# Attention loop: the stage lists of the five engines laid out in another order

## The chip, the cores and the metric

The kernel runs on one core of a Trainium2 chip. The metric is the time of one execution on the device in microseconds, the median of several runs. Each engine (TensorE or PE, VectorE or DVE, ScalarE or ACT, GpSimd or POOL, SyncE or SP, which here only issues DMAs) works through its own instructions in order; they meet only through semaphores.

## What is computed

32 sequences of 512 tokens go through one transformer layer with 256 channels. Cut to what matters:

```python
h = take(emb, x) + (take(lora_A, x) @ lora_B.T) * 2              # embedding with LoRA
n = layernorm(h)
q, k, v = split(n @ Wqkv + bqkv)                                 # 16 heads of 16 channels
local  = softmax(q @ k.T / 4, masked to |i - j| <= 64) @ v
glob   = softmax(q @ k[:64].T / 4) @ v[:64]
gate   = sigmoid(n @ Wg + bg)
h = h + ((1 - gate) * local + gate * glob) @ Wout + bout
f = layernorm(h)
probs, idx = top_2(softmax(f @ router_w.T))                      # 8 experts, weights normalised
# rank of each (token, choice) within its expert, in order over all tokens; a capacity per expert
out = h + sum_k probs_k * expert[idx_k](f)                       # silu(f @ w1) @ w2, kept ranks only
```

## The kernel before

A setup block (to about 50 us) brings weights and tables into place. Then one block runs the attention loop for all 32 sequences, and a last block runs the experts over the slots of a table that the loop has filled. The change lies in the loop alone.

The loop is written as *stages*. ORDER has one list for each engine; an entry is (flag, stage, argument). The function order walks over i from -3 to 34 and yields each entry for sequence i + REL[flag], where that is one of the 32; REL gives old -3, past -2, prev -1, cur 0, nxt 1, far 2, next 3. So an engine works on up to seven sequences at once, and its list is the one thing that sets the order of its work. All waits are on counts that follow from stage and sequence, wherever the stage stands.

The stages, as the text names them (the numbers are the arguments; g is one of four groups of heads):

- *embed, lora 0-1* (PE; ACT and DVE behind them): tokens' LoRA rows are transposed (L824), multiplied (L830) and added to the gathered rows into h (DVE L1138). embed waits for all 8 *gathers* of its sequence (POOL L570, L573). *hold 0-3* (POOL L602) and *hold*, *hb* (SP) keep h for later. *stats1, std1* (ACT square root, L946), *rstd1, scale1* are the first layernorm; *zgate 0-1* (DVE L1175, L1180), *gate*, *gate1*, *gate2*, *gates* the gate.
- *xn_t 0-1, qk 0-3, values 0-2* (PE L837, L843, L781): projections. q and k are split into three bf16 terms: ACT qk (L933), DVE qk (L1099, frees the PSUM bank), ACT qk2 (L940), POOL qk3 (L596), and written out and loaded again by SP (*qk_write*, *load*).
- *max 0-19* (PE scores L685, L701, L707; DVE row maxima L966, L970), five for each g; *cut (g, 0-3)* (DVE) splits the maxima, *m_rows g* (PE L793, ACT L907) turns them, *m_out, m_in* (SP) bring them behind Q. Each max on PE waits for the DVE part of the max before it.
- *exp 0-19* (PE scores L727, L734; ACT exponentials L879, L883): each exp on PE waits for the ACT part of the exp before it. *sel* (POOL L556 and L558, two instructions each) cuts the local ones to the band. *out 0-11* (PE L755, L760) multiplies by the values; *evac* (ACT L889) empties the result.
- *mix 0-3*: PE transposes (L803, both PSUM banks of psX), DVE takes reciprocal, coefficient and product (L1065, L1070, L1075), POOL adds (L589). *attn_t 0-1* (PE L810) waits for all four. *project 0-1* (PE L817, DVE L1120) gives h1; *stats2, std2* (ACT square root, L943), *rstd2, scale2 0-3* (DVE L1161) the second layernorm; *x2_t, router* (PE L850, L857) the router; *residual* (POOL L606), *y*, *x2* (SP) the results.
- *top 0-8, rank 0-5* (DVE): the two best experts and the ranks. top 3 is L1009; top 5 to 8 add up bf16 counts (L1020); *ahead* (PE L864, L865) sums over partitions. rank 4 (L1050 to L1052) writes slot_i and entry and first waits until all *scatters* (POOL L580) of the sequence before have landed; rank 5 is L1055. scatter 0-7 write the slot table and wait for rank 4 of their own sequence.

The PSUM banks of psX (two) go in turn to the PE stages other than exp, max and out, so a stage waits for whoever emptied the bank two stages earlier: embed waits for DVE's project 0.

Of the kernel before, what the change touches and what calls it, by code (L numbers as in the profile page):

```python
# [90 lines left out]
def build(nc, x, emb, lora_a, lora_b, wqkv, bqkv, wout, bout, wg, bg, rw, w1, w2, y):  # L91
# [20 lines left out]
    with outer:  # L112
# [241 lines left out]
        with ExitStack() as mem:  # L354
# [34 lines left out]
            mix = tmp("mix", [P, 2, 2, H, HD])  # L389
# [71 lines left out]
                ("prev", "out", 11), ("cur", "m_rows", 1), ("cur", "values", 2), ("cur", "max", 11), ("nxt", "xn_t", 0),  # L461
                ("nxt", "xn_t", 1), ("cur", "exp", 0), ("cur", "max", 12), ("nxt", "qk", 0), ("nxt", "qk", 1), ("cur", "max", 13),
                ("nxt", "qk", 2), ("nxt", "qk", 3), ("cur", "exp", 1), ("cur", "max", 14), ("prev", "mix", 0), ("cur", "exp", 2),
                ("cur", "max", 15), ("cur", "exp", 3), ("prev", "mix", 1), ("cur", "max", 16), ("cur", "exp", 4), ("cur", "out", 0),
                ("cur", "max", 17), ("prev", "mix", 2), ("cur", "exp", 5), ("cur", "out", 1), ("cur", "exp", 6), ("cur", "max", 18),
# [6 lines left out]
                ("prev", "x2_t", 0), ("nxt", "max", 6), ("cur", "exp", 16), ("cur", "out", 8), ("nxt", "max", 7), ("prev", "x2_t", 1),  # L472
                ("cur", "exp", 17), ("nxt", "max", 8), ("prev", "router", None), ("cur", "exp", 18), ("nxt", "values", 0),
                ("nxt", "max", 9), ("cur", "exp", 19), ("nxt", "values", 1), ("cur", "out", 9), ("nxt", "max", 10), ("cur", "out", 10),
            )
            ORDER["act"] = (
                ("nxt", "qk2", 1), ("prev", "evac", (3, 0)), ("prev", "evac", (3, 1)), ("nxt", "qk", 2), ("nxt", "qk", 3),
                ("nxt", "qk2", 2), ("cur", "exp", 1), ("nxt", "qk2", 3), ("cur", "exp", 2), ("cur", "exp", 3), ("cur", "exp", 4),
                ("cur", "exp", 5), ("cur", "exp", 6), ("cur", "m_rows", 2), ("cur", "exp", 7), ("cur", "evac", (0, 0)),
                ("cur", "evac", (0, 1)), ("cur", "exp", 8), ("cur", "m_rows", 3), ("prev", "attn_t", 0), ("prev", "attn_t", 1),  # L480
                ("cur", "exp", 9), ("far", "embed", None), ("cur", "exp", 10), ("cur", "evac", (1, 0)), ("nxt", "gate", None),
                ("cur", "exp", 11), ("cur", "exp", 12), ("prev", "std2", None), ("cur", "exp", 13), ("cur", "evac", (1, 1)),
                ("cur", "exp", 14), ("cur", "exp", 15), ("nxt", "m_rows", 0), ("cur", "exp", 16), ("prev", "x2_t", 0),
                ("prev", "x2_t", 1), ("cur", "exp", 17), ("cur", "exp", 18), ("cur", "evac", (2, 0)), ("cur", "evac", (2, 1)),
                ("far", "std1", None), ("cur", "exp", 19), ("nxt", "values", 0), ("nxt", "values", 1), ("nxt", "m_rows", 1),
                ("nxt", "values", 2), ("far", "xn_t", 0), ("far", "xn_t", 1), ("far", "qk", 0), ("nxt", "exp", 0),
                ("prev", "weights", None), ("far", "qk", 1), ("far", "qk2", 0),
            )
            ORDER["dve"] = (
                ("nxt", "rstd1", None), ("cur", "cut", (1, 0)), ("cur", "kg", 1), ("cur", "cut", (1, 1)), ("old", "rank", 3),  # L490
                ("nxt", "scale1", 0), ("cur", "cut", (1, 2)), ("cur", "gate1", None), ("cur", "kg", 2), ("cur", "cut", (1, 3)),
                ("old", "rank", 4), ("cur", "max", 10), ("nxt", "scale1", 1), ("nxt", "scale1", 2), ("nxt", "scale1", 3),
# [1146 lines left out]
```

## Time and profile before

| | us |
|---|---|
| median of 3 runs (3838.16 to 3849.77) | 3839.25 |
| the profiled execution | 3837.03 |
| its span | 3834.7 |
| PE busy | 3447.8 (90%) |
| DVE busy | 2241.1 (58%) |
| ACT busy | 1988.1 (52%) |
| POOL busy | 2337.5 (61%) |
| attention loop, about | 50 to 2249 |
| one sequence in the middle | 65.9 |

The busy shares are means over two unlike parts: in the loop (up to about 2250 us) all engines are between 60 and 90% busy, behind it TensorE alone is nearly full. Windows of the loop show more than the page's shares. In a timeline row the bracket tells how long the engine stood idle before it and what released it.

### The profile page before, as it was taken

How to read it: one execution, taken by the hardware profiler on the slowest of the kernel's cores; microseconds unless marked ns; L12 is line 12 of the kernel's file. 1: busy time of each engine (PE TensorE's matmuls, PEld its weight loads, DVE VectorE, ACT ScalarE, POOL GpSimd, SP SyncE). 2: the span in 40 equal slices, each digit the busy share in tenths (PEclk: the TensorE clock that was granted, in tenths of full speed). 3: DMA queues.
4: the chain of work that ended last, by engine and by line, in shares of the span. 5: the costliest groups of instructions: out<-in, count | busy, mean ns of one | idle time of the engine just before them, and what ended most of it. 6: DMA issues, size and time to landing. Idle time of an engine off the chain costs nothing. (4 is left out here: it accounts for less than half of the span.)

```text
span 3834.7 us, 117863 instructions
## 1 busy us (share of the span) xinstructions
PE 3447.8 (90%) x47729; PEld 2806.7 (73%) x47729; DVE 2241.1 (58%) x5390; ACT 1988.1 (52%) x3118; POOL 2337.5 (61%) x2663
## 2 busy tenths in 40 slices
PE   2889898889899898888889739999999999999998
PEld 1565565656565555566565539999999999999998
DVE  3577777777867777777777534443444444343343
ACT  0566665666666666656666524444444444444443
POOL 5467777777777777777776644444444455444443
PEclk7899999999999999999999869999999999999999
DMA  4444444444444544444544223232323333222222
GB/s 138 146 143 154 129 146 144 131 148 137 148 134 146 139 147 134 145 146 130 152 135 148 66 86 59 52 66 49 72 48 70 58 60 74 45 51 45 46 45 41
DMA packets 242539, 398.30 MB, mean 104 GB/s; under 512 B 34572, under 2 KB 150748, under 8 KB 242044
## 3 DMA queue, kind: packets, MB, share of 16 engines
q1 hardware_dynamic: 168540, 297.43, 24.9%
q0 software_dynamic: 70512, 91.16, 13.5%
q8 instruction: 345, 5.65, 0.7%
q10 hardware_dynamic: 3008, 2.95, 0.2%
q14 instruction: 134, 1.10, 0.1%
HBM read 198.55 MB, written 192.88 MB: 102 GB/s over the span
## 5 line engine op out<-in xcount | busy, mean ns | idle before, releaser
L1351 POOL DMA_INDIRECT out_y<-out_t,tok_out x264 | 424.9, 1609 | 732.6 <-DMA out_y<-out_t,tok_out 397.9
L1497 ACT ACTIVATE act<-psS 128x512 f32<-128x512 f32 x528 | 316.0, 599 | 870.7 <-PE psS L1425 870.7
L1559 DVE TENSOR_TENSOR h_lo<-act,h_hi 128x512 fp32r<-128x512 f32 x528 | 367.4, 696 | 553.0 <-ACT h_hi L1498 553.0
L879 ACT ACTIVATE pl<-psS 128x896 f32<-128x896 f32 x512 | 468.4, 915 | 281.2 <-PE psS L727 275.5
L1460 PE MATMUL psO<-w_hi,h_hi 128*128 128x256 f32 x2112 | 598.5, 283 | 0.0
L1460 PE MATMUL psO<-w_lo,h_hi 128*128 128x256 f32 x2112 | 588.7, 279 | 0.0
L1460 PE MATMUL psO<-w_hi,h_lo 128*128 128x256 f32 x2112 | 587.6, 278 | 0.0
L556 POOL TENSOR_SCALAR_AFFINE_SELECT pl<-pl 128x512 f32<-128x512 f32 x512 | 354.8, 693 | 361.8 <-ACT pl L879 360.8
L1425 PE MATMUL psS<-xg_hi,w_hi 128*128 128x256 f32 x1984 | 551.6, 278 | 0.0
L1425 PE MATMUL psS<-xg_hi,w_lo 128*128 128x256 f32 x1984 | 551.3, 278 | 0.0
L1425 PE MATMUL psS<-xg_lo,w_hi 128*128 128x256 f32 x1984 | 551.2, 278 | 0.0
L966 DVE TENSOR_REDUCE negm<-psS 128x4 f32<-128x640 f32 x512 | 416.8, 814 | 196.1 <-PE psS L701 190.8
L1460 PEld LDWEIGHTS psO<-w_hi,h_hi 128*128 128x128 f32 x2112 | 397.1, 188 | 0.0
L1460 PEld LDWEIGHTS psO<-w_lo,h_hi 128*128 128x128 f32 x2112 | 397.0, 188 | 0.0
L1460 PEld LDWEIGHTS psO<-w_hi,h_lo 128*128 128x128 f32 x2112 | 395.5, 187 | 0.0
L1425 PEld LDWEIGHTS psS<-xg_hi,w_hi 128*128 128x128 f32 x1984 | 375.0, 189 | 0.0
L1425 PEld LDWEIGHTS psS<-xg_lo,w_hi 128*128 128x128 f32 x1984 | 372.5, 188 | 0.0
L1425 PEld LDWEIGHTS psS<-xg_hi,w_lo 128*128 128x128 f32 x1984 | 372.4, 188 | 0.0
L1591 DVE TENSOR_SCALAR out_t<-psO,wt_all 128x256 f32<-128x256 f32 x264 | 127.7, 484 | 356.5 <-PE psO L1460 355.5
L558 POOL TENSOR_SCALAR_AFFINE_SELECT pl<-pl 128x512 f32<-128x512 f32 x512 | 328.1, 641 | 0.0
L1498 ACT ACTIVATE h_hi<-psS 128x512 fp32r<-128x512 f32 x528 | 313.1, 593 | 0.0
L1316 POOL DMA_INDIRECT xg<-x_rows,tok_in x245 | 258.5, 1055 | 74.9 <-issue 73.7
(229 smaller groups left out, 7741.8 us busy)
## 6 DMA issues: line engine op xcount, KB each, us to landing
qk_scr<-qk SPq DMA_DIRECT2D x64, 768.0 KB, 4.0
Q<-qk_scr SPq DMA_DIRECT2D x128, 384.0 KB, 4.7
K<-qk_scr SPq DMA_DIRECT2D x128, 384.0 KB, 5.5
qk_scr<-qk SPq DMA_DIRECT2D x64, 512.0 KB, 3.4
qk_scr<-qk SPq DMA_DIRECT2D x64, 256.0 KB, 3.5
h_rows<-held SPq DMA_DIRECT2D x32, 512.0 KB
hb<-h_rows SPq DMA_DIRECT2D x32, 512.0 KB
out_y<-h SPq DMA_DIRECT2D x32, 512.0 KB
```

Of the source, the lines that this page charges most:

```text
L556: pool.affine_select(out=cols[:, :, 0:P], in_=cols[:, :, 0:P], compare_op=ALU.is_ge, fill=0.0, base=0, pattern=[[0, 4], [1, P]], channel_m ...
L558: pool.affine_select(out=cols[:, :, P:WIN], in_=cols[:, :, P:WIN], compare_op=ALU.is_ge, fill=0.0, base=0, pattern=[[0, 4], [-1, P]], chan ...
L879: act.activation(pl[:, v, half, :, lo:hi], psS[:, 0:2, lo:hi], ACT.Exp, scale=SCALE).then_inc(exp_done, 1)
L966: dve.tensor_reduce(negm[:, g, 0, v, :, 2 * half:2 * half + 2], psS[:, 2:4, 0:2 * BAND].rearrange("p a (q u) -> p a q u", u=BAND), AX.X, A ...
L1316: pool.indirect_dma_start(out=rows[:, s, :], out_offset=None, in_=x2_rows[:, :], in_offset=bass.IndirectOffsetOnAxis(ap=tokens[:, s:s + 1] ...
L1351: pool.indirect_dma_start(out=y[:, :], in_=out_t[:, tile.out, s, :], in_offset=None, out_offset=bass.IndirectOffsetOnAxis(ap=tok_out[:, ti ...
L1425: last = pe.matmul(psS[:, f // 2, (f % 2) * 256:(f % 2) * 256 + cols], w[:, tile.par, k, fs], x[:, k, 0:cols], start=(k == 0 and n == 0), ...
L1460: last = pe.matmul(psO[:, s, 0:D], h_[:, f, ts], w[:, tile.par, f, :], start=(f == 0 and n == 0), stop=(f == FT - 1 and n == 2))
L1497: act.activation(act32[:, b, :, 0:cols], src, ACT.Silu)
L1498: act.activation(h_hi[:, 2 * b:2 * b + 2, 0:cols], src, ACT.Silu).then_inc(silu_done, 1)
L1559: dve.tensor_tensor(h_lo[:, 2 * b:2 * b + 2, 0:cols], act32[:, b, :, 0:cols], h_hi[:, 2 * b:2 * b + 2, 0:cols].bitcast(F32), ALU.subtract) ...
L1591: dve.tensor_scalar(out_t[:, tile.out, s, :], psO[:, s, 0:D], wt_all[:, bass.ds(tile.h0 + s, 1)], None, ALU.mult).then_inc(out_done, 1)
```

## The change

All five lists of ORDER are replaced by lists with the same stages in another order. The periods are also cut at other places, which changes only the flags. Nothing else in the kernel changes. The parts that the text below speaks of (whole new list of DVE but for its middle, the first half of PE's and POOL's, the region of std2 in ACT's):

```diff
             ORDER["pe"] = (
...
-                ("nxt", "xn_t", 1), ("cur", "exp", 0), ("cur", "max", 12), ("nxt", "qk", 0), ("nxt", "qk", 1), ("cur", "max", 13),
-                ("nxt", "qk", 2), ("nxt", "qk", 3), ("cur", "exp", 1), ("cur", "max", 14), ("prev", "mix", 0), ("cur", "exp", 2),
...
-                ("cur", "m_rows", 2), ("cur", "exp", 7), ("cur", "max", 19), ("prev", "mix", 3), ("cur", "out", 2), ("cur", "exp", 8),
-                ("cur", "out", 3), ("cur", "m_rows", 3), ("prev", "attn_t", 0), ("prev", "attn_t", 1), ("cur", "exp", 9),
-                ("past", "ahead", None), ("prev", "project", 0), ("prev", "project", 1), ("far", "embed", None), ("nxt", "max", 0),
-                ("cur", "exp", 10), ("cur", "out", 4), ("nxt", "max", 1), ("cur", "exp", 11), ("far", "lora", 0), ("nxt", "max", 2),
-                ("cur", "exp", 12), ("cur", "out", 5), ("nxt", "max", 3), ("cur", "exp", 13), ("far", "lora", 1), ("nxt", "max", 4),
-                ("cur", "exp", 14), ("cur", "out", 6), ("cur", "out", 7), ("nxt", "max", 5), ("cur", "exp", 15), ("nxt", "m_rows", 0),
...
+                ("nxt", "xn_t", 1), ("cur", "exp", 0), ("cur", "max", 12), ("nxt", "qk", 0), ("cur", "exp", 1), ("nxt", "qk", 1),
+                ("cur", "exp", 2), ("nxt", "qk", 2), ("cur", "max", 13), ("nxt", "qk", 3), ("cur", "exp", 3), ("cur", "max", 14),
+                ("prev", "mix", 0), ("cur", "exp", 4), ("cur", "max", 15), ("cur", "out", 0), ("prev", "mix", 1), ("cur", "exp", 5),
+                ("cur", "max", 16), ("cur", "exp", 6), ("cur", "m_rows", 2), ("cur", "max", 17), ("prev", "mix", 2),
+                ("cur", "max", 18), ("cur", "exp", 7), ("cur", "out", 1), ("prev", "mix", 3), ("cur", "max", 19), ("cur", "exp", 8),
+                ("cur", "out", 2), ("cur", "exp", 9), ("cur", "out", 3), ("past", "ahead", None), ("cur", "m_rows", 3),
+                ("nxt", "max", 0), ("prev", "attn_t", 0), ("prev", "attn_t", 1), ("nxt", "max", 1), ("cur", "exp", 10),
+                ("prev", "project", 0), ("nxt", "max", 2), ("cur", "exp", 11), ("prev", "project", 1), ("far", "embed", None),
+                ("cur", "out", 4), ("cur", "exp", 12), ("nxt", "max", 3), ("far", "lora", 0), ("cur", "exp", 13), ("nxt", "max", 4),
+                ("cur", "out", 5), ("far", "lora", 1), ("nxt", "max", 5), ("cur", "exp", 14), ("cur", "out", 6), ("cur", "out", 7),
...
             ORDER["act"] = (
...
+                ("prev", "exp", 11), ("nxt", "embed", None), ("prev", "exp", 12), ("past", "std2", None), ("prev", "exp", 13),
...
             ORDER["dve"] = (
...
+                ("old", "rank", 1), ("cur", "max", 0), ("old", "rank", 2), ("cur", "max", 1), ("old", "rank", 3), ("prev", "kg", 3),
+                ("cur", "kg", 0), ("old", "rank", 4), ("cur", "max", 2), ("past", "project", 0), ("past", "project", 1),
+                ("past", "stats2", 0), ("past", "stats2", 1), ("cur", "max", 3), ("old", "rank", 5), ("nxt", "lora", 0),
+                ("past", "rstd2", None), ("cur", "max", 4), ("past", "scale2", 0), ("cur", "cut", (0, 0)), ("past", "scale2", 1),
+                ("cur", "cut", (0, 1)), ("cur", "max", 5), ("past", "scale2", 2), ("nxt", "lora", 1), ("past", "scale2", 3),
+                ("cur", "max", 6), ("cur", "cut", (0, 2)), ("cur", "cut", (0, 3)), ("cur", "max", 7), ("nxt", "stats1", 0),
...
+                ("nxt", "scale1", 2), ("past", "top", 3), ("cur", "max", 10), ("past", "top", 4), ("nxt", "scale1", 3),
+                ("cur", "gate1", None), ("cur", "max", 11), ("cur", "kg", 1), ("nxt", "zgate", 0), ("cur", "kg", 2),
+                ("cur", "max", 12), ("past", "top", 5), ("past", "top", 6), ("nxt", "qk", 0), ("nxt", "qk", 1), ("cur", "max", 13),
+                ("nxt", "qk", 2), ("past", "top", 7), ("nxt", "qk", 3), ("cur", "max", 14), ("prev", "mix", (0, 0)),
...
             ORDER["pool"] = (
...
+                ("old", "scatter", 6), ("prev", "mix", 3), ("cur", "sel", 7), ("old", "scatter", 7), ("far", "gather", 7),
+                ("nxt", "hold", 2), ("cur", "sel", 8), ("past", "scatter", 0), ("nxt", "hold", 3), ("cur", "sel", 10),
...
+                ("prev", "residual", 3), ("nxt", "sel", 0), ("far", "qk3", 0), ("nxt", "sel", 1), ("far", "qk3", 1),
+                ("nxt", "sel", 2), ("far", "qk3", 2), ("far", "qk3", 3), ("next", "gather", 4), ("next", "gather", 5),
+                ("nxt", "sel", 3), ("past", "scatter", 5), ("nxt", "sel", 5), ("cur", "mix", 0), ("cur", "mix", 1),
+                ("nxt", "sel", 6), ("far", "hold", 1), ("next", "gather", 6), ("cur", "mix", 2),
             )
             ORDER["sp"] = (
...
+                ("cur", "y", None), ("cur", "x2", None), ("next", "qk_write", (0, 0)), ("far", "m_in", 1),
```

## Rows read from the trace of the kernel before

**Rows 1.** Windows: busy us of PE, PEld, DVE, ACT, POOL; granted clock; DMA.

```profile
1226.59:1292.50 65.91, 59.79 (x1077) 39.39 (x1076) 49.63 (x127) 40.82 (x60) 49.01 (x65) 0.95 0.50 140
2200.00:3834.00 1634.00, 1551.18 (x13309) 1546.26 (x13308) 655.41 (x1326) 679.78 (x1237) 763.49 (x586) 0.97 0.30 57
```

**Rows 2.** Timeline of PE (start, length, what): exp 0 and embed.

```profile
1226.59 0.46 PE L727 MATMUL psS<-Q,K 102*32 102x96 bf16 x16
...
1261.32 0.60 PE L824 MATMUL psX<-ident,la 128*16 128x128 f32 x4
```

**Rows 3.** Window from qk to the last mix; DVE and POOL in it.

```profile
1230.10:1254.60 24.50, 20.44 (x373) 12.50 (x375) 22.90 (x47) 13.82 (x22) 19.61 (x24) 0.93 0.52 175
...
1230.80 1.21 DVE L1175 TENSOR_TENSOR xn_wg<-xn,wg_b 128x1024 f32<-128x1024 f32 x1
...
1234.45 0.97 DVE L1009 TENSOR_TENSOR onehot<-iota,top_f 128x64 f32<-128x64 f32 x1
...
1246.96 2.40 DVE L1020 TENSOR_TENSOR before<-before,chosen 128x8 bf16<-128x8 bf16 x1
...
1248.71 0.62 POOL L558 TENSOR_SCALAR_AFFINE_SELECT pl<-pl 128x512 f32<-128x512 f32 x1
```

**Rows 4.** PE at max 19; window behind it, columns as in the first group.

```profile
1250.15 0.79 PE L707 MATMUL psS<-K,Q 96*128 96x64 bf16 x16 [1.69 <-DVE negm L966]
1250.75 1.95 PE L803 MATMUL psX<-ident,o_t 128*128 128x128 f32 x8
...
1250.60:1254.10 3.50, 3.50 (x23) 2.07 (x24) 2.55 (x11) 0.60 (x1) 1.50 (x2) 0.53 0.79 228
```

**Rows 5.** Timeline: ACT from exp 12 to exp 13, PE at exp 14.

```profile
1266.09 0.92 ACT L879 ACTIVATE pl<-psS 128x896 f32<-128x896 f32 x1 [0.94 <-PE psS L727]
1267.03 1.28 ACT L943 ACT_TABLE_LOAD   x1
...
1269.93 0.92 ACT L879 ACTIVATE pl<-psS 128x896 f32<-128x896 f32 x1
...
1270.99 1.06 PE L734 MATMUL psS<-Q,KG 102*64 102x512 bf16 x4 [1.73 <-ACT pl L879]
```

**Rows 6.** Timeline of POOL: qk3, two selects; grouped: mix (mean ns of one).

```profile
1233.07 2.27 POOL L596 TENSOR_TENSOR qk<-qk_rest,qk 128x512 bf16<-128x512 f32 x2
...
1240.80 0.63 POOL L556 TENSOR_SCALAR_AFFINE_SELECT pl<-pl 128x512 f32<-128x512 f32 x1
...
1241.98 0.64 POOL L556 TENSOR_SCALAR_AFFINE_SELECT pl<-pl 128x512 f32<-128x512 f32 x1
...
L589 POOL TENSOR_TENSOR attn<-mix 128x256 f32<-128x256 f32 x28 | 20.1, 731 | 15.0 <-DVE mix L1075 14.8
```

**Rows 7.** Timeline: last scatter and slot_i at the end; last gather and embed at the start.

```profile
2234.06 0.97 POOL L580 DMA_INDIRECT slot_table<-entry,slot_i  x1 [0.30 <-issue]
...
2238.47 0.17 DVE L1050 TENSOR_TENSOR slot_i<-slot,over 128x8 int32<-128x8 f32 x1 [9.46 <-DMA slot_table<-entry,slot_i]
...
60.18 0.95 POOL L573 DMA_INDIRECT emb_t<-in_L_tok_emb_weight,id_cur  x1 [0.30 <-issue]
...
63.01 1.02 PE L824 MATMUL psX<-ident,la 128*16 128x128 f32 x4 [19.10 <-DMA emb_t<-in_L_tok_emb_weight,id_cur]
```

**Rows 8.** DVE and PE behind embed: project, max 0 to out 4, x2_t; window.

```profile
1261.52 0.69 DVE L1120 TENSOR_TENSOR h<-psX,hb 128x512 f32<-128x512 f32 x1 [1.03 <-PE psX L817]
1261.85 0.46 PE L685 MATMUL psS<-K,Q 96*32 96x96 bf16 x16
1262.47 0.99 PE L755 MATMUL psO<-pl,V 128*32 128x256 f32 x16
1263.98 0.82 DVE L966 TENSOR_REDUCE negm<-psS 128x4 f32<-128x640 f32 x1 [0.68 <-PE psS L701]
...
1275.62 0.66 PE L850 MATMUL psX<-ident,x 128*128 128x128 f32 x4
...
1261.50:1272.80 11.30, 9.57 (x236) 6.09 (x238) 10.04 (x24) 8.89 (x12) 8.90 (x16) 0.92 0.29 88
```

More of the change, by code:

```diff
@@ L473, in build @@
-                ("cur", "exp", 17), ("nxt", "max", 8), ("prev", "router", None), ("cur", "exp", 18), ("nxt", "values", 0),
-                ("nxt", "max", 9), ("cur", "exp", 19), ("nxt", "values", 1), ("cur", "out", 9), ("nxt", "max", 10), ("cur", "out", 10),
+                ("prev", "exp", 19), ("prev", "out", 9), ("cur", "values", 1), ("cur", "max", 10), ("prev", "out", 10),
+                ("cur", "m_rows", 1), ("prev", "out", 11), ("cur", "values", 2), ("cur", "max", 11), ("nxt", "xn_t", 0),
@@ new lines, in build @@
+                ("cur", "out", 4), ("cur", "exp", 12), ("nxt", "max", 3), ("far", "lora", 0), ("cur", "exp", 13), ("nxt", "max", 4),
+                ("cur", "out", 5), ("far", "lora", 1), ("nxt", "max", 5), ("cur", "exp", 14), ("cur", "out", 6), ("cur", "out", 7),
+                ("cur", "exp", 15), ("nxt", "max", 6), ("prev", "x2_t", 0), ("prev", "x2_t", 1), ("cur", "exp", 16),
+                ("nxt", "max", 7), ("nxt", "m_rows", 0), ("cur", "out", 8), ("cur", "exp", 17), ("prev", "router", None),
@@ L480, in build @@
[L480 to L487, printed above, removed]
+                ("prev", "m_rows", 3), ("past", "attn_t", 0), ("past", "attn_t", 1), ("prev", "exp", 10), ("prev", "evac", (0, 1)),
@@ L488, in build @@
+                ("cur", "exp", 8), ("cur", "evac", (0, 0)), ("cur", "exp", 9),
             )
             ORDER["dve"] = (
[L490 to L492 removed]
@@ L501, in build @@
-                ("cur", "gates", None), ("prev", "mix", (3, 1)), ("cur", "cut", (3, 2)), ("cur", "kg", 3), ("cur", "cut", (3, 3)),
-                ("prev", "mix", (3, 2)), ("past", "rank", 0), ("past", "rank", 1), ("prev", "project", 0), ("prev", "project", 1),
-                ("nxt", "max", 0), ("nxt", "max", 1), ("prev", "stats2", 0), ("nxt", "max", 2), ("prev", "stats2", 1),
-                ("far", "lora", 0), ("nxt", "max", 3), ("prev", "rstd2", None), ("prev", "scale2", 0), ("nxt", "kg", 0),
@@ L509, in build @@
+                ("cur", "cut", (3, 1)), ("prev", "mix", (3, 2)), ("cur", "cut", (3, 2)), ("cur", "cut", (3, 3)),
+                ("past", "rank", 0),
             )
             ORDER["pool"] = (
-                ("cur", "sel", 8), ("nxt", "hold", 1), ("nxt", "hold", 2), ("nxt", "hold", 3), ("cur", "sel", 10), ("cur", "sel", 11),
-                ("old", "scatter", 4), ("cur", "sel", 12), ("cur", "sel", 13), ("next", "gather", 0), ("next", "gather", 1),
-                ("next", "gather", 2), ("old", "scatter", 5), ("old", "scatter", 6), ("old", "scatter", 7), ("cur", "sel", 15),
@@ L514, in build @@
-                ("prev", "residual", 0), ("cur", "sel", 16), ("cur", "sel", 17), ("next", "gather", 3), ("prev", "residual", 1),
-                ("cur", "sel", 18), ("prev", "residual", 2), ("prev", "residual", 3), ("nxt", "sel", 0), ("far", "qk3", 0),
-                ("far", "qk3", 1), ("past", "scatter", 0), ("far", "qk3", 2), ("far", "qk3", 3), ("nxt", "sel", 1), ("nxt", "sel", 2),
-                ("nxt", "sel", 3), ("next", "gather", 4), ("cur", "mix", 0), ("cur", "mix", 1), ("next", "gather", 5), ("nxt", "sel", 5),
@@ L518, in build @@
-                ("nxt", "sel", 6), ("cur", "mix", 2), ("next", "gather", 6), ("next", "gather", 7), ("cur", "mix", 3), ("nxt", "sel", 7),
-                ("past", "scatter", 1), ("far", "hold", 0), ("past", "scatter", 2), ("past", "scatter", 3),
+                ("old", "scatter", 6), ("prev", "mix", 3), ("cur", "sel", 7), ("old", "scatter", 7), ("far", "gather", 7),
+                ("nxt", "hold", 2), ("cur", "sel", 8), ("past", "scatter", 0), ("nxt", "hold", 3), ("cur", "sel", 10),
+                ("cur", "sel", 11), ("past", "scatter", 1), ("cur", "sel", 12), ("cur", "sel", 13), ("past", "scatter", 2),
```

49 lines of the change are left out of this document (25 added, 24 removed).

## The prediction, made before the changed kernel was seen

> **What bounds the kernel now.** I read the page's first lines, then the stretches, then one sequence of the attention loop as a timeline of each engine. The loop over 32 sequences ends near 2250 us; the expert stage behind it has TensorE busy nearly throughout and is not touched [rows 1]. One sequence in the middle takes 65.9 us from its first scores, exp 0 at 1226.59, to the next sequence's [rows 1, 2]. TensorE is busy 59.8 of them at a mean granted clock of 0.95, so 6.1 us are waits and, at full clock, some 3.3 us more would fall away: 9.4 us a sequence, 290 us in all, is the most that an order can give. No other engine is full: DVE 49.6, POOL 49.0, ACT 40.8 us [rows 1]. What counts is who waits for whom, and where.
>
> Two places carry most of the loss. First, from the q and k projections to the last mix DVE is busy 22.9 of 24.5 us, while TensorE has 20.4 at a clock of 0.93: there DVE sets the pace [rows 3]. It does work there that nothing near waits for: zgate's product (1.21 us), top 3 (0.97), rank 5, and an 8-element addition, top 7, that lasts 2.40 us, from 1246.96 until the fourth of four select instructions on POOL ends (1249.33) [rows 3]. Behind it max 19 starts after 1.69 us of idle TensorE, and the mix after it takes 1.95 us, at the lower of the two clock levels (0.53 of full over 3.5 us, 1.2 GHz nearly throughout) [rows 4]. Second, ACT takes a square root between exp 12 and exp 13: two table loads of 1.28 us, and so exp 14 on TensorE starts after 1.73 us of idle [rows 5].
>
> **The change part by part.** Every stage, wait and buffer stays; no instruction is added. So the sum is one of positions. I count from exp 0 of a sequence.
>
> *First stretch, exp 0 to embed: before 34.7 us* (1226.59 to 1261.32 [rows 2]). The new DVE list takes zgate 0 ahead of it, zgate 1 between max 16 and 17, top 3 and 4 ahead, and rank 5 behind max 3; of the rows named 2.2 us leave the full piece (1.21 + 0.97), and rank 5 and the short parts 1, 2 and 4 of top with them. DVE then is no longer what is late; POOL is. In the new list POOL runs, from its first qk3 (6.5 us after exp 0 [rows 6]) on, without a pause: 4 qk3 of 1.14, the selects 1, 2, 3, 5, 6, 7 at 1.18 from start to start, 4 additions of mix and 1 of hold (of the same size) at 0.73 [rows 6], and 3 gathers and 3 scatters at 0.97 + 0.30 of issue [rows 7]. That is 4.6 + 7.1 + 3.7 + 7.6 = 23.0 us in all, and scatter 7 of the sequence three back is done on POOL at 29.5.
>
> Here the order makes a wait that costs nothing today. rank 4 of the next sequence overwrites the entries, and so waits until all eight scatters have landed. Before, it stands at the end of the period, with POOL four selects, four residuals and a gather beyond scatter 7; now it stands behind max 1, ahead of max 2 and both projects. The landing has a row: the last of eight scatters ends on POOL at 2235.03, and DVE's slot_i starts at 2238.47, 3.4 us later [rows 7]. So rank 4 can start at 32.9, and its three operations (0.17 and two like it, overlapped: some 0.4), max 2 (0.82) and project 0 (0.69 [rows 8]) end at 34.8. Behind DVE in rank 4 stand max 2, for which TensorE waits at max 3, and project 0, which frees embed's bank: embed at 34.8. A second path ends close by: embed also waits for the last gather, now right behind scatter 7, at 29.5 + 1.27 + 1.9 = 32.7 (gather end 61.13 to embed 63.01 [rows 7]). Embed thus comes when it did, 34.8 against 34.7, but max 0, exp 10, max 1, exp 11 and max 2 are now ahead of it. A max with an exp takes 0.62 us there (1261.85 to 1262.47 [rows 8]), so this is 0.62 + 0.62 + 0.4 = 1.6 us of work already done.
>
> *Second stretch, embed to the next exp 0: before 31.2 us.* Off come the 1.6. Off comes the wait at exp 14: between exp 13 and exp 14 TensorE had lora 1 and max 4, and now has max 4, out 5, lora 1 and max 5, about 3 us, while the root waits where it did; what is late next there is nothing, since exp 13 ends on ACT about 3.8 us after exp 12 (1267.01 to 1270.85 [rows 5]) and TensorE gets to exp 14 later than that: -1.7. On comes a wait at x2_t. From project 1 to the fourth scale2 DVE is busy 10.0 us today [rows 8]; the new list has three max (0.82 each) and a copy for KG less there, and rank 5 and one max more: some 8.8 us, which with small waits of its own (0.7, my guess) puts x2 at 44.3. TensorE gets there from embed in 14.3 us today (1261.32 to 1275.62 [rows 8]); less the 1.6, the 1.7 and the 1.6 that the low clock costs (below) that is 9.4, so 44.2, and I take +0.4 for the uncertainty of both. The other moves here (out 11 behind m_rows 1, router behind exp 17, evac (3, 0) ahead of the next sequence) have covers of over a microsecond on both sides and I cost them at nothing; if the covers fail, they are the 0.3 us waits that stand in such places now.
>
> *Clock and stalls.* The clock falls behind the 1.7 us idle of max 19 (0.53 over 3.5 us [rows 4]), and the stretch behind embed has 0.92 on the whole [rows 8]. A stretch like the first costs 3.5 x (1 - 0.53) = 1.6 us. A shorter idle may leave the clock up (-1.6 a sequence), and DVE's short operations will now meet other POOL work: top 7 stands beside qk3 and selects, the first coefficient of mix beside qk3. No row shows the new meetings. They are bounded below by 0 and above by the 2.40 us row once in the piece that carries the path plus 1.14 (a whole qk3) once, so 0 to 3.5; I take 0.8 for both together, since POOL and not DVE is late there by the sum above, and the clock gives part back.
>
> By the Trainium skill (SBUF — State Buffer, section "Who interferes with whom") a DVE instruction with two SBUF inputs and a GpSimd one that reads SBUF exclude each other, and the second to issue waits until the first is done. By that rule top 7 would wait for one select, 0.64 us, or one qk3, 1.14 [rows 6]; the row in [rows 3] shows the exclusion, but a wait through four selects. By the rule alone the upper end of the stalls would be 2.3 and not 3.5 us.
>
> Sum for one sequence: 34.8 + 31.2 - 1.6 - 1.7 + 0.4 + 0.8 = 63.9, against 65.9: -2.0. All lists are full for about 28 of the 32 sequences (the flags span seven, and the first and last have stages missing): -56 us.
>
> *The end of the loop.* Here the same edit gains. Before, rank 4 of the last but one sequence comes behind the last one's router, so the last one's slot_i waits 9.46 us for those scatters [rows 7]. The new list has it ahead of the last one's project; its scatters 0 to 4 go out before and 5 to 7 just behind the last residuals, and the wait shrinks to some 0.5: -9 us. The start shows no such thing: the same gathers and loads bound it, 0 +- 3.
>
> The profiled execution took 3837.0 us, its span 3834.7; the median of the runs is 3839.25, 2.2 more. 3837.0 - 56 - 9 = 3772, as a median 3774.
>
> **The rivals.**
> (a) *More goes than the sum says.* If POOL keeps up with the new queue (today it has pauses in it), the two large waits simply go, with what the low clock costs behind the first: 65.9 - 1.7 - 1.6 - 1.7 and 0.8 of stalls is 61.7. 28 x -4.2 - 9 = -127: 3712. For it: DVE and ACT are both relieved where they were late. Against: rank 4 stands there, and its price has a row.
> (b) *Given back.* The wait of DVE in rank 4, with all that is queued behind it, takes the place of that at max 19 and exp 14: period 65.9, and only the end gains: 3830.
> (c) *Slower.* The same wait is longer than what was won. It works through POOL: each microsecond by which mix 3 is late there (DVE's mix stalled by selects, as top 7 was) moves sel 7, scatter 7, its landing, rank 4, max 2 and embed one for one. It decides from 2.3 us of lateness a sequence beyond my sum (2.0, and 0.3 for the end). With the upper bound of the stalls (3.5 instead of 0.8) and the x2_t wait a little longer (0.2) the period is 66.8: 28 x 0.9 - 9 = +16: 3855. For it: DVE finishes its mixes within a microsecond or two of POOL. Against: DVE sheds 4 us there.
> (d) *It doesn't do what it says.* The lists could be mere rotations. They are not: rank 4 goes some 40 places up on DVE against its neighbours.
>
> **How the numbers follow.** Forecast 0.50, (a) 0.20, (b) 0.13, (c) 0.15, (d) or other 0.02. A measurement of this kernel can tell about 0.3% (12 us) from no change; (b) lies within. Faster 0.72, same 0.13, slower 0.15. The range takes in most of (a) and all of (b), and leaves (c)'s upper part: 3710 to 3855.
>
> **What would show it.** Right: period 63 to 65; no idle of over 1 us at max 19 or exp 14; DVE idle before slot_i in each sequence with the landing of slot_table as its releaser, or POOL without a pause from qk3 to scatter 7; embed about 35 us after exp 0; the 9.46 us wait gone; granted clock in the loop at or over 0.96. Wrong: rank 4 waiting over 3 us (then (c)), or embed well ahead of 34 us (then (a)); or DMA-bound loads of Q and K, which my sum takes as in time because their places on SP move by less than their present slack.

## The result, and the profile after

The changed kernel takes 3718.18 us (median of 4 runs, 3716.92 to 3719.01), the kernel before 3844.51 (4 runs, 3838.16 to 3853.59): ratio 0.967, 95% interval 0.965 to 0.969. I had forecast 3774, so the sign and the range hold. The range was wide, from a clear gain to no gain at all, and the point is 56 us too high: the gain is 126 us and not 65, about that of rival (a), 3712.

The experiments ran elsewhere. The record names chip 13 for the first eight runs (I call it the second chip: the kernel before takes 4042 to 4045 us there and the changed one 3786) and chip 0 for the last four, from the spread run on (the third chip: the kernel before takes 4028, the changed one was not run). For the two kernels above it names no chip; I call theirs the first. The kernels are the same to the letter, so I put the 5% between 3844 and 4042 down to the chips, which is an inference. I keep them apart: the first for what the change did in my prediction's terms, the others for causes.

Where the 118 us between the two profiled executions went (first chip; exp 0 of the first and of the last sequence, then the end):

| | before | after | difference |
|---|---|---|---|
| start to the first exp 0 | 126.5 | 124.3 | -2.2 |
| first exp 0 to the last | 2013.3 | 1912.7 | -100.6 |
| last exp 0 to the end of the span | 1694.9 | 1679.5 | -15.4 |
| one sequence (mean of 22 in the middle) | 66.05 | 62.23 | -3.82 |

The same window of the kernel before, from the first exp 0 to the last (us from and to, length, busy time of PE, PEld, DVE, ACT, POOL, granted clock, DMA share, GB/s):

```profile
126.50:2139.80 2013.30, 1800.78 (x33238) 1197.66 (x33241) 1505.04 (x3828) 1261.41 (x1814) 1483.37 (x1969) 0.97 0.47 142
```

And of the kernel after, with one sequence in the middle, which answers to [rows 1]:

```profile
124.30:2037.00 1912.70, 1775.01 (x33238) 1157.86 (x33241) 1576.79 (x3842) 1239.79 (x1815) 1470.06 (x1973) 0.99 0.53 149
1233.65:1295.73 62.08, 57.48 (x1078) 37.53 (x1077) 52.35 (x128) 40.30 (x60) 48.69 (x65) 1.00 0.53 150
```

DVE is busier by 72 us in a shorter loop, and it costs nothing: its share is not what sets the time. The granted clock went from 0.97 to 0.99. In the clock records of the loop TensorE stood at 1.2 GHz for 133 us before (31 stretches, 30 of them in or right behind the wait at max 19 or at exp 14) and for 34 us after (9 stretches). That is 67 us of full-clock time lost before and 17 after.

The timeline of TensorE in that sequence of the kernel after, for [rows 2, 4, 5, 8]: mix 1, exp 6, mix 3, embed and x2_t (start, length, what, then in brackets the idle time before it and what ended it):

```profile
1248.11 1.09 PE L807 MATMUL psX<-ident,o_t 128*128 128x128 f32 x8 [0.53 <-DVE mix L1079]
...
1250.61 0.46 PE L731 MATMUL psS<-Q,K 102*32 102x96 bf16 x16 [0.62 <-ACT pl L883]
...
1256.68 1.09 PE L807 MATMUL psX<-ident,o_t 128*128 128x128 f32 x8 [1.35 <-DVE mix L1079]
...
1269.77 0.60 PE L828 MATMUL psX<-ident,la 128*16 128x128 f32 x4
...
1279.36 1.09 PE L854 MATMUL psX<-ident,x 128*128 128x128 f32 x8
```

The waits of 1.69 us at max 19 and of 1.73 at exp 14 are gone, embed comes 36.1 us after exp 0, and x2_t starts with no idle. The longest wait left is a new one, 1.35 us at mix 3. DVE and POOL show where it comes from and what became of rank 4:

```profile
1252.65 0.67 POOL L562 TENSOR_SCALAR_AFFINE_SELECT pl<-pl 128x512 f32<-128x512 f32 x1
1253.25 1.44 POOL L593 TENSOR_TENSOR attn<-mix 128x256 f32<-128x256 f32 x2
1253.97 1.93 DVE L1074 TENSOR_TENSOR coef<-rsum,gates 128x32 f32<-128x32 f32 x1
1254.62 0.65 POOL L560 TENSOR_SCALAR_AFFINE_SELECT pl<-pl 128x512 f32<-128x512 f32 x1
1255.21 0.64 POOL L562 TENSOR_SCALAR_AFFINE_SELECT pl<-pl 128x512 f32<-128x512 f32 x1
...
1263.00 1.01 POOL L584 DMA_INDIRECT slot_table<-entry,slot_i  x1 [0.16 <-issue]
...
1267.48 0.17 DVE L1054 TENSOR_TENSOR slot_i<-slot,over 128x8 int32<-128x8 f32 x1
```

The product coef for part 2 (32 elements, mix (2, 1) in the list) took 1.93 us, through POOL's second mix addition and two selects. It stands where top 7 stood before ([rows 3], 2.40 us). Scatter 7 ends at 1264.01 (1263.00 + 1.01), rank 4 runs at 1267.48: 3.5 us later.

At the end of the loop (DVE, the last slot_i; before it waited 9.46 us [rows 7]):

```profile
2126.36 0.17 DVE L1054 TENSOR_TENSOR slot_i<-slot,over 128x8 int32<-128x8 f32 x1 [0.35 <-DMA slot_table<-entry,slot_i]
```

### The profile page after: what moved, and what is told of

Same layout as the page of the kernel before. It is cut to its first block and busy times, and to the rows that moved or that the text cites. A ratio compares the mean times of both kernels' runs of the same rounds, so it can differ in the third digit from the quotient of the medians.

```text
span 3716.5 us, 117861 instructions
## 1 busy us (share of the span) xinstructions
PE 3422.8 (92%) x47729; PEld 2766.8 (74%) x47729; DVE 2313.3 (62%) x5390; ACT 1964.8 (53%) x3116; POOL 2321.8 (62%) x2663
## 5 line engine op out<-in xcount | busy, mean ns | idle before, releaser
L560 POOL TENSOR_SCALAR_AFFINE_SELECT pl<-pl 128x512 f32<-128x512 f32 x512 | 330.0, 644 | 162.6 <-ACT pl L883 157.3
L562 POOL TENSOR_SCALAR_AFFINE_SELECT pl<-pl 128x512 f32<-128x512 f32 x512 | 328.9, 642 | 0.0
L584 POOL DMA_INDIRECT slot_table<-entry,slot_i x256 | 258.2, 1008 | 98.2 <-DVE entry L1056 55.9
```

The source lines that it names most:

```text
L560: pool.affine_select(out=cols[:, :, 0:P], in_=cols[:, :, 0:P], compare_op=ALU.is_ge, fill=0.0, base=0, pattern=[[0, 4], [1, P]], channel_m ...
L562: pool.affine_select(out=cols[:, :, P:WIN], in_=cols[:, :, P:WIN], compare_op=ALU.is_ge, fill=0.0, base=0, pattern=[[0, 4], [-1, P]], chan ...
L584: pool.indirect_dma_start(out=table[:, :], in_=entry[:, q, k, :], in_offset=None, out_offset=bass.IndirectOffsetOnAxis(ap=slot_i[:, q, k:k ...
```

## The experiments

**What had to be told apart.** Theory: the loop gained by the two waits and, as a price of its own, by the clock that no longer falls behind them; the early rank 4 matters at the end only. Rivals: the waits alone; a floor elsewhere. The first group of four runs overturned the plan, because on the second chip other waits dominate.

**The cover of exp 14 alone** (kernel before, TensorE's list):

```diff
-("nxt","max",3), ("cur","exp",13), ("far","lora",1), ("nxt","max",4), ("cur","exp",14), ("cur","out",6), ("cur","out",7), ("nxt","max",5)
+("nxt","max",3), ("cur","exp",13), ("nxt","max",4), ("cur","out",5), ("far","lora",1), ("nxt","max",5), ("cur","exp",14), ("cur","out",6), ("cur","out",7)
```

> The kernel before with one piece of the new TensorE list: max 4, out 5, lora 1 and max 5 stand ahead of exp 14 (before: lora 1 and max 4). Nothing else moves. Theory (waits and the clock behind them are two prices): the 1.7 us wait at exp 14 goes in about 29 sequences, -50 us, and with it the some ten stretches at half clock that follow it, 10 x 1.7 = -17 us: 3839 - 67 = 3772. Rival one (my prediction's own step, the wait only, the clock comes down elsewhere): -1.7 x 28 = -48, 3791. Rival two (given back: with exp 14 on time the next wait, x2_t or exp 15, takes it over): 3825 or more.

Measured: 4063.4 us against 4045.5, ratio 1.005 (1.002 to 1.007). Both theories of a gain miss. Rival two gave the number (nothing gained) but not the mechanism: exp 14 isn't on time, it starts at 46.9 us of the sequence (median) where it was at 43.0. What holds it is the other engine's list, shown with the spread run with both moves below.

**top 7 and 8 behind max 19 alone** (kernel before, DVE's list):

```diff
-("prev","mix",(2,2)), ("past","top",7), ("cur","max",18), ("past","top",8), ("cur","max",19)
+("prev","mix",(2,2)), ("cur","max",18), ("cur","max",19), ("past","top",7), ("past","top",8)
```

> The kernel before with one move on DVE: top 7 and top 8 stand behind max 19 instead of around max 18. Nothing else moves. Theory: the 2.4 us addition no longer holds max 18 and 19, TensorE's 1.7 us wait at max 19 goes (-47 us over 28 sequences) and with it some twenty stretches at half clock, 48 us of TensorE's time in all: 3839 - 95 = 3744. Rival one (the wait only): 3792. Rival two (the locked addition just moves: mix 3 and the transposes behind it wait instead, and the clock falls there): 3825 or more.

Measured: 4035.3, ratio 0.998 (0.996 to 0.999). Nearly nothing, and the trace of the kernel before on this chip (below) says why: there the same top 7 takes 1.24 us and not 2.40, since POOL's selects fall differently, and max 19 waits 0.2 us at most. So rival two's number holds here for want of a wait to take away, not by its mechanism. What the move would give on the first chip isn't shown by it.

**Both** (the two edits above together):

> The kernel before with both moves: exp 14 covered on TensorE, top 7 and 8 behind max 19 on DVE. Four stages of some 190 change places. Theory: the two places are independent and all the loop's gain is in them: 3839 - 67 - 95 = 3677, below the changed kernel's 3718. Rival one (a common floor: DVE from the q and k projections to the last mix holds the period near the 62.2 us of the changed kernel): 31 x -2.7 = 3755. Rival two (clock: half clock comes back behind any of the smaller waits once the large ones are gone): only the two waits, 3839 - 97 = 3742.

Measured: 4057.8, ratio 1.004 (1.002 to 1.005). All three expectations miss, for the reasons of the first two runs.

**The early rank undone** (changed kernel; DVE's rank 4 and 5 behind router, POOL's scatters 0 to 4 later):

```diff
-("cur","kg",0), ("old","rank",4), ("cur","max",2) ... ("cur","max",3), ("old","rank",5) ... ("past","router",None)
+("cur","kg",0), ("cur","max",2) ... ("cur","max",3) ... ("past","router",None), ("old","rank",4), ("old","rank",5)
-("cur","sel",18), ("next","gather",2), ("past","scatter",4), ("next","gather",3)
+("cur","sel",18), ("past","scatter",0), ("next","gather",2), ("past","scatter",1), ("next","gather",3), ("past","scatter",2)
```

> The changed kernel with the early rank undone: rank 4 and 5 stand behind router on DVE, and scatters 0 to 4 move some 20 us later on POOL, as they must. Theory (the early rank matters at the end only): the loop keeps its 62.2 us period within 0.3, the wait of the last slot_i for the scatters of the sequence before comes back (some 9 us), so 3718 + 9 = 3727, up to 3733 if all of the end's gain goes. Rival (rank 4 with its landing holds embed in every sequence, as my prediction's chain said): with it gone embed comes about 1 us earlier and the period falls by 0.5 to 1: 3718 - 14 to -28 + 9, about 3705.

Measured: 3960.3, ratio to the kernel before 0.981 (0.978 to 0.983). To be read beside the changed kernel on the same chip, 3786: 174 us lost, where 9 were expected. Its last slot_i waits 10.21 us, as the theory says (0.13 in the changed kernel on this chip), but the loop lost 6 us a sequence, which no theory had.

**The changed kernel, and the kernel before, again, on the second chip:**

> The changed kernel once more, unaltered, beside the kernel before on the chip that also runs the next three. In the first group of runs the kernel before took 4045 us, not 3844, and TensorE had idle times that end with nothing but its own issue, some 6 us a sequence. If that group's chip hands TensorE its instructions more slowly, the ratio of the changed kernel to the kernel before there is open: 0.967 if the stalls cost both the same, lower if the waits that the change takes away were also there. On a chip like the first: 3718 within 5 us, ratio 0.967.

> The kernel before once more, unaltered, for its trace on this chip. If the chip is like the first: period 66, TensorE without waits that end with its own issue (11.6 us in all at the exp matmuls). If it is like that of the first group: period above 72, with some 6 us a sequence of idle that ends with issue, in the same stretch behind exp 12.

Measured: 3786.1 against 4042.0, ratio 0.937 (0.934 to 0.939), so the change is worth nearly twice as much there. The kernel before has a period of 72.3 us instead of 66.1, the changed one 64.2 instead of 62.2. One stretch of the kernel before explains it (timeline, of it POOL and some of TensorE):

```profile
1232.58 0.96 POOL L573 DMA_INDIRECT emb_t<-in_L_tok_emb_weight,id_cur  x1 [0.30 <-issue]
1233.37 0.30 PE L727 MATMUL psS<-Q,K 102*32 102x96 bf16 x5 [0.46 <-issue]
1233.85 0.95 POOL L570 DMA_INDIRECT la<-lora_rows,id_cur  x1 [0.30 <-issue]
...
1234.12 0.28 PE L727 MATMUL psS<-Q,K 102*32 102x160 bf16 x4 [0.45 <-issue]
...
1234.87 0.23 PE L727 MATMUL psS<-Q,K 102*32 102x160 bf16 x1 [0.47 <-issue]
1235.10 1.01 POOL L580 DMA_INDIRECT slot_table<-entry,slot_i  x1 [0.30 <-issue]
...
1235.59 0.25 PE L727 MATMUL psS<-Q,K 102*32 102x160 bf16 x2 [0.49 <-issue]
...
1236.41 1.00 POOL L580 DMA_INDIRECT slot_table<-entry,slot_i  x1 [0.30 <-issue]
1237.00 0.27 PE L793 MATMUL psX<-identb,m_cut 128*24 128x128 bf16 x2 [1.10 <-issue]
...
1237.71 0.97 POOL L580 DMA_INDIRECT slot_table<-entry,slot_i  x1 [0.30 <-issue]
1238.45 0.47 PE L850 MATMUL psX<-ident,x 128*128 128x128 f32 x1 [0.34 <-issue]
```

POOL issues six indirect DMAs one after the other (gathers 0, 1, 2, scatters 5, 6, 7; 7.5 us), and one exp, 16 matmuls that take 0.45 us elsewhere, comes in pieces of 4 (not shown), 5, 4, 1 and 2 with pauses that nothing ends but TensorE's own issue. The waits view sums them: on the second chip first, then the same line on the first chip (us in total, times, longest).

```profile
PE psS L727 <- issue: 58.4, 130, 1.9
```

```profile
PE psS L727 <- issue: 11.6, 30, 1.3
```

I summed the pauses of over 0.45 us between the starts of two weight loads of one line, inside and up to 1.5 us behind such a run: 3.98 us a run on the second chip, 0.2 on the first. The changed kernel has no run longer than three; on the second chip it is 0.61 a run of three, 0.37 a run of two.

**The cover of exp 14 undone in the changed kernel:**

```diff
-("cur","exp",13), ("nxt","max",4), ("cur","out",5), ("far","lora",1), ("nxt","max",5), ("cur","exp",14), ("cur","out",6), ("cur","out",7)
+("cur","exp",13), ("far","lora",1), ("nxt","max",4), ("cur","exp",14), ("cur","out",5), ("cur","out",6), ("cur","out",7), ("nxt","max",5)
```

> The changed kernel with the cover of exp 14 undone: out 5 and max 5 stand behind exp 14 again and lora 1 ahead of max 4, as in the kernel before. Theory (wait and clock are two prices): exp 13 ends on ACT at 42.6 us of the sequence, TensorE reaches exp 14 at 41.5, so 1.1 to 1.7 us of idle a sequence, of which some comes back since max 5 and out 5 are then still to do beside the next waits: +1.3 x 28 = +36, and half clock behind it in a third of the sequences, +17: 0.014 over the changed kernel. Rival (my prediction's step, the wait and nothing more): +1.2 x 28 = +34, 0.009. Rival (there is slack): 0 to 0.002.

Measured: 3859.8, ratio to the kernel before 0.955 (0.952 to 0.958), against 0.937: 74 us, 2.4 a sequence. Three waits of TensorE in one sequence of it (exp 14, max 6, x2_t):

```profile
1215.74 0.62 PE L739 MATMUL psS<-Q,KG 102*64 102x512 bf16 x4 [1.59 <-ACT pl L884]
...
1220.18 0.45 PE L690 MATMUL psS<-K,Q 96*32 96x160 bf16 x16 [0.64 <-DVE negm L971]
...
1221.43 1.09 PE L855 MATMUL psX<-ident,x 128*128 128x128 f32 x8 [0.67 <-DVE x L1166]
```

That is more than any of the three gave (0.014 is 53 us). The clock is not the reason, it hardly fell (5 us lost in the whole loop of the changed kernel, 9 here). The wait costs more than itself, since max 5 and out 5, now behind it, push max 6 and x2_t into waits too: 1.59 + 0.64 + 0.67 = 2.9, 2.4 of which reach the period. So the cover is worth over 2 us a sequence on this chip, more than the 1.7 of my sum.

**top 7 back at its old place in the changed kernel:**

```diff
-("nxt","qk",2), ("past","top",7), ("nxt","qk",3) ... ("prev","mix",(2,2)), ("cur","max",18)
+("nxt","qk",2), ("nxt","qk",3) ... ("prev","mix",(2,2)), ("past","top",7), ("cur","max",18)
```

> The changed kernel with one move undone on DVE: top 7 stands between the mix of part 2 and max 18 again, beside POOL's select and mix instructions. Theory: the 8-element addition waits there for the run of POOL instructions in progress, 1.2 to 2.4 us, holds max 18 and 19, and TensorE waits at max 19 or mix 3; with the half clock behind it +1.5 to +3 us a sequence: ratio to the changed kernel 1.011 to 1.022. Rival (the addition finds POOL in a gather or scatter there and takes 0.3): +0.002 or less. Rival (clock is no own price): the wait alone, 1.009 at most.

Measured: 3783.7, ratio to the kernel before 0.936 (0.934 to 0.938), the same as the changed kernel. The first rival holds: top 7 takes 0.15 us there (22.9 us after exp 0), between POOL's hold 1, which ends at 22.9, and gather 6 from 23.1. The place in DVE's list costs nothing as such; what counts is what POOL does at that moment. So no run shows that moving top 7 is what removed the wait at max 19; the new lists as a whole did.

**POOL's run spread, alone, in the kernel before:**

```diff
-("next","gather",0), ("next","gather",1), ("next","gather",2), ("old","scatter",5), ("old","scatter",6), ("old","scatter",7), ("cur","sel",15), ("prev","residual",0), ...
+("next","gather",0), ("old","scatter",5), ("cur","sel",15), ("next","gather",1), ("prev","residual",0), ("old","scatter",6), ("cur","sel",16), ("cur","sel",17), ("next","gather",2), ("prev","residual",1), ("old","scatter",7), ("cur","sel",18), ("next","gather",3), ...
```

> The kernel before with POOL's list alone changed: the run of six indirect DMAs without a pause (gathers 0, 1, 2 and scatters 5, 6, 7) is spread between the selects and residuals that follow it, so that no more than two stand together. In the kernel before on this chip TensorE's weight loads falter inside such a run, 4.0 us a run, waiting for nothing but their own issue; on the first chip 0.2 us a run. Theory A (a run of indirect DMAs holds back TensorE's instructions): the stalls go, 4 us and the waits and half clock that come of them, -5 to -7 us a sequence: 4042 - 190 = 3850, within 50. Theory B (the number of indirect DMAs counts, or what else runs there): 4042 within 20. Theory C (the chip is slower at something else and the run only happens to lie there): 4042 within 20.

Measured: 3858.9 against 4028.4, ratio 0.957 (0.956 to 0.959). Theory A, within 9 us: the same six DMAs, with selects and residuals between them; both kernels ran on the third chip. The trace of the kernel before that I compare with is the second chip's (4042 against 4028 us). Against it the period falls from 72.3 to 66.1, that of the first chip; the waits from 11.3 to 7.5 us a sequence and what the low clock takes from 4.4 to 0.9.

**The spread run with the two moves:**

> The kernel before with the same spreading on POOL and the two moves of the run with both (exp 14 covered by out 5, lora 1 and max 5; top 7 and 8 behind max 19). Theory A (these three places are the loop's gain): the two moves now show what they are worth, 1.7 + 1.7 us of waits and 1.5 of half clock a sequence: 130 us under the spread kernel alone, some 3730, below the changed kernel's 3786 on such a chip. Rival (floor): once they go, DVE or the evictions hold the period near 64 and the kernel ends within 20 us of the changed one, 3770 to 3810. Rival (the two moves are worth nothing, as in the first group of runs): within 15 us of the spread kernel.

Measured: 3994.0, ratio 0.992 (0.990 to 0.994): 135 us slower than the spread run without them. All three expectations miss. The trace shows the fault of my edit (TensorE and DVE, timeline):

```profile
1217.65 2.08 PE L836 MATMUL psX<-lb_t,la_t 128*128 128x256 f32 x4
...
1219.77 0.69 DVE L1144 SCALAR_TENSOR_TENSOR h<-psX,emb_t 128x512 f32<-128x512 f32 x1 [3.58 <-PE psX L836]
...
1220.37 1.21 DVE L976 TENSOR_REDUCE negm<-psS 128x16 f32<-128x1024 f32 x1
...
1221.73 0.43 PE L691 MATMUL psS<-K,Q 96*32 96x96 bf16 x14 [2.01 <-DVE negm L976]
```

DVE's list still has lora 1 ahead of max 4. With lora 1 behind max 4 and out 5 on TensorE, DVE idles 3.58 us for it, reads max 4's scores only then, and max 5, which needs their bank and now stands ahead of exp 14, waits 2.01 us. exp 13 is done at 43.3 us, exp 14 starts at 48.0. The changed kernel has lora 1 behind max 5 on DVE too. The run with the cover alone shows the same chain (max 5 at 45.5, behind max 4 on DVE, done at 45.4). So these runs don't price the cover; the undone one does.

**A run of five in the changed kernel, rank 4 staying early:**

```diff
-("cur","sel",18), ("next","gather",2), ("past","scatter",4), ("next","gather",3)
+("cur","sel",18), ("past","scatter",0), ("next","gather",2), ("past","scatter",1), ("next","gather",3), ("past","scatter",2)
```

(and scatters 3 and 4 behind qk3 1 and gather 5, as in the run with the late rank)

> The changed kernel with POOL's list alone changed: scatters 0 to 4 stand where the run with the late rank had them, so that five indirect DMAs follow one another (scatter 0, gather 2, scatter 1, gather 3, scatter 2). Rank 4 stays early on DVE. Theory A (the run is the cost of the kernel with the late rank, 3960 against 3786): 3950 within 20, with TensorE's weight loads faltering 3.4 us in each run. Rival (the late rank on DVE is the cost): 3786 within 15.

Measured: 3965.4, ratio 0.985 (0.982 to 0.987). Theory A. The changed kernel was not run on this chip, so I compare ratios to the kernel before: 0.985 here, 0.981 with the late rank, 0.937 for the changed kernel. The late places of the scatters alone thus bring back all of that loss, and the place of rank 4 adds none in the loop. The pauses themselves are 3.0 us of the 6.5 by which the period is longer (70.7 against 64.2); the waits in all are 9.4 us a sequence against 5.2, the low clock takes 1.9 against 0.1. A piece of one run:

```profile
1223.21 1.59 PE L759 MATMUL psO<-pl,V 128*32 128x256 f32 x10
1223.83 0.98 POOL L577 DMA_INDIRECT emb_t<-in_L_tok_emb_weight,id_cur  x1 [0.30 <-issue]
1225.11 1.01 POOL L584 DMA_INDIRECT slot_table<-entry,slot_i  x1 [0.30 <-issue]
1225.59 0.54 PE L759 MATMUL psO<-pl,V 128*32 128x192 f32 x5 [0.79 <-issue]
```

At the end the two differ in the direction that the prediction's chain says. The last slot_i, with the late rank (second chip) and then with the early one but late scatters (third chip):

```profile
2362.31 0.17 DVE L1055 TENSOR_TENSOR slot_i<-slot,over 128x8 int32<-128x8 f32 x1 [10.21 <-DMA slot_table<-entry,slot_i]
```

```profile
2366.00 0.17 DVE L1054 TENSOR_TENSOR slot_i<-slot,over 128x8 int32<-128x8 f32 x1 [3.38 <-DMA slot_table<-entry,slot_i]
```

**The remaining gaps treated in the changed kernel:**

```diff
-("cur","mix",0), ("cur","mix",1), ("nxt","sel",6), ("far","hold",1), ("next","gather",6), ("cur","mix",2)
+("cur","mix",0), ("next","gather",6), ("cur","mix",1), ("nxt","sel",6), ("far","hold",1), ("cur","mix",2)
-("past","scatter",4), ("next","gather",3), ("prev","residual",1)
+("past","scatter",4), ("prev","residual",1), ("next","gather",3)
-("cur","m_rows",3), ("nxt","max",0), ("prev","attn_t",0), ("prev","attn_t",1)
+("nxt","max",0), ("prev","attn_t",0), ("prev","attn_t",1), ("cur","m_rows",3)
```

> The changed kernel with the waits that are left in its trace treated: gather 6 stands between mix 0 and mix 1 on POOL, so that DVE's 32-element product for part 2 (1.93 us behind mix 1 and a select in two of three sequences) gets in at once; m_rows 3 stands behind the transposes of attn on TensorE and ACT; residual 1 stands between scatter 4 and gather 3. Theory (mix 3's wait of 1.3 us and m_rows 3's go): -1.3 to -1.8 us a sequence, 3786 - 45 = 3741. Rival (the DVE product is caught in another run of POOL work, or exp 6 and exp 9 wait longer instead): within 10 us of 3786.

Measured: 3753.2, ratio to the kernel before 0.932 (0.930 to 0.933) against the changed kernel's 0.937 (0.934 to 0.939) on the second chip: 0.5% faster, if ratios carry from one of these chips to the other. The period is 63.1 against 64.2, less than the theory's 1.3 to 1.8. The product coef, all 128 of them, in the changed kernel on the second chip and in this one (grouped by line: busy time and mean ns of one behind the first bar):

```profile
L1074 DVE TENSOR_TENSOR coef<-rsum,gates 128x32 f32<-128x32 f32 x128 | 91.7, 716 | 3.3
```

```profile
L1076 DVE TENSOR_TENSOR coef<-rsum,gates 128x32 f32<-128x32 f32 x128 | 53.4, 417 | 3.3
```

and, in its timeline:

```profile
1210.27 0.74 POOL L595 TENSOR_TENSOR attn<-mix 128x256 f32<-128x256 f32 x1
1211.17 0.23 DVE L1076 TENSOR_TENSOR coef<-rsum,gates 128x32 f32<-128x32 f32 x1
1211.17 0.97 POOL L576 DMA_INDIRECT la<-lora_rows,id_cur  x1 [0.16 <-issue]
```

With a gather in progress on POOL the product takes 0.23 us, where it took 1.72 in the changed kernel on the second chip, and mix 3 no longer waits. Three moves were made at once, so how much each gave isn't shown.

## Why the prediction was right, and where its sum was off

I divide the 22 middle sequences of both kernels (first chip) as the prediction did, with TensorE's idle time and what the low clock took in each part:

| us a sequence | before | predicted | after |
|---|---|---|---|
| exp 0 to embed | 34.7 (idle 4.3, clock 1.8) | 34.8 | 36.1 (idle 4.2, clock 0.5) |
| embed to the next exp 0 | 31.3 (idle 2.7, clock 0.9) | 28.3 | 26.1 (idle 0.3, clock 0.0) |
| clock and stalls together | | +0.8 | in the two above |
| period | 66.05 | 63.9 | 62.23 |

*What bounds it, and the two waits.* Right. Waits fall by 2.5 us a sequence, the low clock's share by 2.2; 0.9 comes back as busy time of TensorE, which I have not traced.

*rank 4 and POOL's queue.* The chain is right, each time about 1 us late. Forecast: scatter 7 done at 29.5, rank 4 at 32.9, embed at 34.8. Measured (medians of the 22): 30.4, 33.8, 36.1. The last sign of the landing comes 2.7 to 4.7 us after scatter 7 ends on POOL (median 3.7, 25 middle sequences), where the one row that I had gave 3.4. DVE idles for it at rank 4 by 0.4 us in the mean and 1.3 at most, and max 2 is in time: (c) had the right chain and asked for more lateness than there is. In 14 of the 22 sequences embed starts within 0.15 us of the end of project 0, as the chain has it. In the other 8 TensorE gets there 0.3 to 0.7 us later by its own work and the wait at mix 3, which the sum had not placed ahead of embed. So two paths end together at embed, and part of the agreement is luck.

*Exp 14.* Right: no idle. The sum took 1.7 for it. The undone cover puts it at 2.4 on the second chip, with the waits that follow.

*x2_t.* Forecast 0.4 of wait; x2 is done at 45.3, TensorE arrives at 45.6, the wait is 0. My arrival at 44.2 took off the 1.6 of the low clock, which the sum for the period did not. Two small waits that I had left as they were, out 10 (0.31 us a sequence in the mean) and max 7 (0.15), went too.

*Clock and stalls, +0.8.* This term was mis-sized. I lumped them, let them cancel and ended on the side of a cost. Measured apart, the stalls came: mix (2, 1) 1.93 us where it was 0.18, the last cut 0.73 where it was 0.18, rank 3 1.44 where it was 0.77, of which 1.1 us reach TensorE at mix 3 and 0.5 at m_rows 3. That is 1.6 on the path, within my bounds of 0 to 3.5. But the clock gave 2.2, more than the 1.6 that I had named as possible and not counted: -0.6 in place of +0.8. These 1.4 and the 0.4 of x2_t are as large as the gap between 63.9 and 62.2; the 0.5 of the two small waits and the 0.9 of busy time act on it too, in opposite directions. A wait of 1.35 us at mix 3 left the clock up in all 16 middle sequences of the changed kernel that have it; of its nine waits of 1.7 us or more (mix 3 or m_rows 3) six went with a stretch at 1.2 GHz, as did 18 of the 22 waits of 1.7 us (one of 2.4) at max 19 and 11 of the 28 at exp 14 before. The length of the wait doesn't settle it: one of 1.10 us at max 19 (fifth sequence, before) was followed by such a stretch too. The trace of before has 30 of 31 such stretches at the two waits that the change takes away, so taking them away should have taken the stretches off the sum as well.

*The Trainium skill's rule* ("SBUF — State Buffer", "Who interferes with whom") stands beside this: an exclusive lock, held for one instruction. The exclusion shows again. Its length doesn't fit: the product issued at 1253.97 got in at 1255.90, behind one mix addition and two selects, and at once when POOL's next instruction was a gather.

*The end.* Forecast -9. The wait went from 9.46 to 0.35, as said (0.5). The span's end gains 15.4: the first matmul of the expert stage comes 11.4 us earlier after the last exp 0 (112.4 instead of 123.8), and 3.5 more come between that and the first matmul on the gathered rows (120.2 instead of 135.1). What gives these 3.5 isn't traced.

*The late rank as the price of the end.* On the second chip the last slot_i waits 10.21 us with it and 0.13 in the changed kernel, and from the last exp 0 to the end of the span it is 1695.7 against 1685.4 us. The run of five DMAs shows that the scatters' places count as well: with the early rank but late scatters the wait is 3.38 us and the end takes 1694.6 (third chip).

*What my reading of the kernel before could not show.* The run of six indirect DMAs on POOL. On the first chip it cost 0.2 us, and no rival named it; on the second it is 6.2 of the 8.1 us a sequence that the change gains (72.3 to the spread kernel's 66.1 on the third, then 64.2), since the new list breaks it up. So the ratio of 0.967 belongs to the first chip, and for the second the explanation is another one.

**Open.** How much the two waits and the clock are worth on the first chip one by one, since no experiment ran there: there the cause is read from the two traces, and the wait at max 19, which the second chip doesn't have, was priced by no run at all. What in a run of indirect DMAs holds TensorE back. Why the first measurement and the other two chips differ in it, and whether it is the chips at all.

## What to carry to other kernels

When a wait goes, take the stretch at half clock behind it off the sum as well, if the clock rows put it there; and price stalls and clock apart. When a stage is moved on one engine's list, move its partner on the engine that frees its buffer: the same cover was worth 2.4 us a sequence with its partner (second chip), and the spread run that had it without its partner lost 4 (third chip). Keep indirect DMAs apart on POOL's list, no more than two together, with compute between them: on one chip the run of six cost 0.2 us, on another spreading it was worth 170 us in all.

## What the runs showed of the hardware

*A run of indirect DMAs on POOL holds back TensorE's issue.* Pauses of about 0.7 us recur from about 1 us after the run's start (3.5 in the run of five) until about 1 us after its end. In sum they are 4.0 us in a run of six in the kernel before on the second chip, 3.9 with top 7 moved and 2.9 with exp 14 covered; 3.0 and 3.4 in one of five; 0.4 to 0.6 in one of three; and 0.2 in a run of six on the first chip. Spreading a run took the time back, and making one in the changed kernel lost it again. The transfers of the instruction queue (345 of 16 KB in either kernel, 1.19 us each on the first chip and 1.21 on the second) are no slower, and where one landed inside a run the pauses went on behind it. By the Trainium skill ("Runtime: NRT & Kernel Launch", "Instruction fetch mechanics") instructions are fetched ahead and the fetch is mostly hidden; beside a single indirect DMA the trace agrees (0.0 to 0.2 us of pauses), in a run of six it has 4.0 us. Whether these pauses are waits for instructions no run shows.

*The same kernel took 3844, 4042 and 4028 us on three chips* (the first not named in the record), and the same change of order was worth 3.3% on the first and 6.3% on the second.

*How long DVE and POOL exclude each other depends on when they meet.* In 25 middle sequences of the changed kernel mix (2, 1) took 1.92 to 1.93 us in 16, 2.5 to 2.6 in 4, and 0.64 to 0.73 in 5; in those 5 the last cut behind it took 2.04 instead of 0.73, and m_rows 3 waited 1.7 us for it. Which of the two is caught depends on some tenths of a microsecond.
